# Four of fifteen row offsets of banded products as two 32x32 tiles in place of one 64x64 tile

## The reference

```python
x = x + L0_conv(ln(x))       # focal modulation: three depthwise convolutions of 3x3, 5x5, 7x7
t = t + L0_ffn(ln(t))        # a recurrence over the tokens: y = sigmoid(Wx + y V')
x = x + L1_conv(ln(x))       # a state-space mixer, forward and backward over the tokens
t = t + L1_ffn(ln(t))        # eight experts, the best two of each token
```

```python
for l, k in enumerate((k0, k1, k2)):
    ctx = gelu(dwconv_same(ctx, k))          # 3x3, then 5x5 on the result, then 7x7
    ctx_all = ctx_all + ctx * gates[..., l:l + 1]
```

## Time and profile before

| | us |
|---|---|
| median of 3 runs | 782.67 |
| lowest and highest run | 780.81 and 787.14 |
| profiled execution | 786.88 |
| span of its trace, first to last instruction | 785.1 |

### The profile page before, as it was taken

One profiled execution on the slowest core, in us unless ns is written; L12 is line 12 of the kernel. 1 busy time (PEld: TensorE's weight loads), 2 busy tenths in 40 slices (PEclk: granted clock), 3 DMA queues, 4 the chain that ended last, 5 costly groups with the idle time before them and its releaser, 6 DMA issues. The chain is left out here.

```text
span 785.1 us, 14059 instructions
## 1 busy us (share of the span) xinstructions
PE 635.6 (81%) x5604; PEld 400.8 (51%) x5610; DVE 623.2 (79%) x669; ACT 360.3 (46%) x567; POOL 470.0 (60%) x239
## 2 busy tenths in 40 slices
PE   7899669977837888888788789789789887885695
PEld 4787436644514555555455455456455554552242
DVE  3376874233319999999999999999999999977765
ACT  2222236653285566556556556556556564322000
POOL 2000000001018999999999999999999999960000
PEclk9999989986986999999999999999999999999777
DMA  9500000000355878779788878787877987800002
GB/s 371 224 3 3 1 2 1 1 2 2 92 121 131 205 199 232 194 201 233 193 199 228 201 202 215 212 203 204 222 201 199 227 202 198 224 14 1 1 12 52
DMA packets 35489, 110.43 MB, mean 141 GB/s; under 512 B 6816, under 2 KB 8992, under 8 KB 35040
## 3 DMA queue, kind: packets, MB, share of 16 engines
q1 hardware_dynamic: 35200, 108.71, 52.0%
q0 software_dynamic: 224, 0.83, 0.3%
HBM read 105.97 MB, written 3.54 MB: 139 GB/s over the span
## 5 line engine op out<-in xcount | busy, mean ns | idle before, releaser
L549 POOL TENSOR_TENSOR ring<-ring,big 128x1152 f32<-128x1152 f32 x74 | 193.7, 2631 | 4.0 <-DVE ring L922 4.0
L196 PE MATMUL banks<-ring,main_params 128*128 128x288 f32 x592 | 173.8, 422 | 0.6 <-POOL ring L549 0.6
L691 ACT ACTIVATE big<-big,small 128x576 f32<-128x576 f32 x192 | 142.5, 765 | 30.4 <-DVE ring L922 15.8
L922 DVE TENSOR_TENSOR_SCAN ring<-big,banks 128x576 f32<-128x576 f32 x111 | 146.1, 1340 | 1.5
L910 DVE TENSOR_TENSOR banks<-banks,big 128x576 f32<-128x576 f32 x192 | 141.2, 743 | 2.7 <-POOL big L535 1.6
L1260 PE MATMUL banks<-big,selectors 96*128 96x512 bf16 x192 | 72.7, 390 | 70.1 <-DVE ring L922 39.9
L196 PEld LDWEIGHTS banks<-ring,main_params 128*128 128x128 f32 x592 | 105.1, 191 | 36.1 <-issue 4.0
L525 POOL COPY big<-normed 128x288 f32<-128x288 f32 x8 | 3.0, 427 | 179.4 <-DVE normed L451 179.4
L549 POOL TENSOR_TENSOR normed<-normed,big 128x1152 f32<-128x1152 f32 x36 | 94.4, 2630 | 0.6 <-DVE normed L922 0.6
L691 ACT ACTIVATE banks<-big,small 128x576 f32<-128x576 f32 x64 | 47.5, 742 | 79.3 <-DVE ring L922 46.3
L196 PE MATMUL banks<-normed,main_params 128*128 128x288 f32 x288 | 83.5, 420 | 0.0
(11 more groups left out here) (186 smaller groups left out, 1002.2 us busy)
## 6 DMA issues: line engine op xcount, KB each, us to landing
big<-bc_rows SPq DMA_DIRECT2D x256, 288.0 KB, 4.4
big<-bc_rows SPq DMA_DIRECT2D x128, 144.0 KB, 4.4
big<-toeplitz_in SPq DMA_DIRECT2D x1, 3584.0 KB, 24.5
big<-toeplitz_in SPq DMA_DIRECT2D x1, 2560.0 KB, 15.2
bc_rows<-big SPq DMA_DIRECT2D x16, 144.0 KB, 3.6
big<-toeplitz_in SPq DMA_DIRECT2D x1, 1536.0 KB, 10.2
residual<-x_in SPq DMA_DIRECT2D x2, 576.0 KB, 5.8
out<-big SPq DMA_DIRECT2D x16, 72.0 KB, 1.8
```

Of the source, the lines that this page charges most:

```text
L196: last = nc.tensor.matmul(PS[rows, 2 * p + a, 0:HALF], lhsT, rhs[:, bass.ds(at + a * HALF, HALF)], start=start, stop=stop, skip_group_chec ...
L549: nc.gpsimd.tensor_tensor(slots, slots, CT[k % 5], ALU.mult).then_inc(weighted, 1)
L691: nc.scalar.activation(out, DT[b % 3], ACT.Exp, scale=ANEG[:, s:s + 1]).then_inc(decay_set, 1)
L922: nc.vector.tensor_tensor_scan(slot, DECAY[m % 3], place, 0.0, ALU.mult, ALU.add).then_inc(scanned, 1)
```

## The change

For four of the fifteen row offsets each 64x64 product is replaced by two 32x32 products, one for each block on the diagonal: strip b of the half's rows, weights of that block, and output partitions 64q + 32b to 64q + 32b + 31. Columns, bank, `start` and `stop` are those of the product replaced. The offsets are given by their place i in the order of `offsets(l)`: the second of level 0 (dy = -1), the third of level 1 (dy = 1), the third and the fifth of level 2 (dy = 1 and 2). All else stays, the layout of the weights in memory too.

```diff
@@ -246,6 +246,7 @@
         LINEAR = {(0, 1): ("q", 0), (1, 0): ("q", 1), (1, 1): ("global", 0), (2, 0): ("global", 1)}
+        SPLIT_AT = [(1,), (2,), (2, 4)]
         LINEARS = list(LINEAR.values())
@@ -1084,7 +1085,14 @@
                         for q in range(2):
                             at = TW_AT[l] + 64 * ((dy + KS[l] // 2) * CP + 2 * k + q)
                             dst = PS[64 * q:64 * (q + 1), 4 * kh + 2 * r + k % 4 // 2, k % 2 * COLS:(k % 2 + 1) * COLS]
-                            last = nc.tensor.matmul(dst.rearrange("p (m y) -> p m y", y=H)[:, :, ys], TW[rows, at:at + 64],
+                            dst = dst.rearrange("p (m y) -> p m y", y=H)[:, :, ys]
+                            if i in SPLIT_AT[l]:
+                                for b in range(2):
+                                    strip = slice(64 * r + 32 * b, 64 * r + 32 * (b + 1))
+                                    last = nc.tensor.matmul(dst[32 * b:32 * (b + 1)], TW[strip, at + 32 * b:at + 32 * (b + 1)],
+                                                            src[strip, 2 * k + q, :, there], start=i == 0, stop=i == KS[l] - 1)
+                                continue
+                            last = nc.tensor.matmul(dst, TW[rows, at:at + 64],
                                                     src[rows, 2 * k + q, :, there], start=i == 0, stop=i == KS[l] - 1)
                 return last
```

## The result

The changed kernel takes 794.23 us (median of 10 runs, 789.24 to 799.07), the kernel before 783.71 us beside it (10 runs, 780.64 to 787.14): a ratio of 1.0143, 95% interval 1.0111 to 1.0175, or 8.7 to 13.7 us more. The forecast was 10.2 us more. The profiled execution of the changed kernel took 799.07 us with a span of 797.3, the slowest of its runs.

What follows compares the result with a forecast made beforehand. TensorE, limited by streamed columns, was taken to bound the bands, with losses arriving whole. One of 32 splits falls into a hole; 31 x 0.33 = 10.2 us, added to the 782.67 median, gives 792.9 us, range 788 to 799.

Steps and rivals of the forecast that it cites:

- the bands: The banded products of L1087, one stretch from 27.6 to 69.4 us, TensorE busy for 41.33 of 41.80 us.
- A microsecond lost in the bands is a microsecond at the end: Behind the bands: nothing absorbs TensorE's loss, so the 10.2 us arrive whole in the total time.
- the stretches after it keep their lengths: Sign for the stages behind the bands: unchanged in length, while the bands' stretch grows from 41.7 to about 52 us.
- Instructions and loads cost nothing of their own: In the split passes: 256 more matmul records and 256 more loads cost no time; shorter loads gain nothing.
- The columns' price: TensorE's streaming in the bands: 0.87 ns a column, from 0.157 us a pass with a mean of 182 columns.
- The price of a split offset: Each split offset in the bands: two changes of tile form plus staggers, 0.11 + 0.06 + 0.13 + 0.03 = 0.33 us.
- The linear product of 41.86: L377 between bands, sixteen 32x32 tiles: same pair of form switches in the earlier trace, 0.38 us lost.
- The cover: The 0.43 us hole before 37.06, a wait for ScalarE's L570, takes up one split's 0.33 us; 31 remain.
- Rival 1, the switch is free: At the split offsets the array need not empty: nothing paid or gained, 782.7 us; chance 0.08.
- Rival 2, two strips take turns: Two strips of one 64-row half write one bank in turn, 0.16 us more per split pass: 803.1 us; chance 0.06.
- Rival 3, the clock: Stalls drop TensorE to 1.2 GHz for a while in the bands, 10 us more, some 803; chance 0.04.
- The estimate of 53 ns a switch: About 128 array cycles of drain at 2.4 GHz; 64 switches cost 3.4 us, 786.1 us in all; forecast rejected it.

Runs made afterwards that it cites:

- the short delay: Kernel before plus 9 idle 128x128 bf16 products ahead of the last half of level 2, bands untouched: ratio 1.0022 (0.9992 to 1.0053).
- the long one: Kernel before plus 44 idle 128x128 bf16 products ahead of the last half of level 2, bands untouched: ratio 1.0166 (1.0133 to 1.0199).
- level 0 alone: Against the kernel before, only the one offset of level 0 split into 32x32 tiles, 8 split offsets in place of 32: 790.69 us, ratio 1.007.
- the kernel with the same record counts and one tile form: Against the kernel before, the same four offsets as two products each, split by streamed columns, all tiles 64x64: 787.32 us, ratio 1.0009.
- all offsets small: Against the kernel before, all fifteen row offsets as two 32x32 tiles, no change of form left in the bands: 804.0 us, ratio 1.0259.
- the adjacent offsets: Changed kernel, but level 2 splits its third and fourth offsets, next to each other, not third and fifth: 793.58 us, ratio 1.0121 against the kernel before.
- one of 64x64 tiles: Against the kernel before, twelve offsets (all but each level's first) as two products each, split by columns, tiles kept 64x64: 802.17 us, ratio 1.021.

## Why the prediction was right

*What bounds the stage, and that the loss arrives whole.* Right in its main part: 9.51 us lost in the bands, a ratio that means 8.7 to 13.7 in the whole. "A microsecond lost in the bands is a microsecond at the end" holds for the short delay and is a little too low for the long one; the surplus of the changed kernel itself (11.2 by the ratio, 10.5 by the medians, against 9.5) is inside the interval. The sign "the stretches after it keep their lengths" did not hold in the profiled execution: the norms took 43.34 us for 41.77, at a lower granted clock, and only the 3 us allowed for the runs covered that. For level 0 alone, the 2.8 to 8.1 us stay unexplained: the short delay, as large in the bands, gave -0.6 to 4.2.

*Instructions and loads cost nothing of their own.* Right at this density, and shown by the kernel with the same record counts and one tile form (ratio 1.0009). The step rested on the spacing of 8 ns within one linear product, though, which is a burst and says nothing of a long run: with all offsets small, twice the instructions in the bands cost 17 us. The columns' price was taken as 0.87 ns; the stretch of eighty records gives 0.157 us / 182 = 0.86, which changes no term.

*The price of a split offset.* Forecast 0.11 + 0.06 + 0.13 + 0.03 = 0.33 us; measured at 38.1 us 0.11 + 0.05 + 0.14 + 0.02 = 0.32, and 0.32 again from the adjacent offsets. By the whole stretch it is (9.51 + 0.32) / 32 = 0.31. The linear product of 41.86 was the same pair of changes, and the only correction that it needed was half the stagger. That the two changes of form differ by 0.03 us matches the loads, 103 against 132 ns. The trace of before has a third length of load, 188 ns, into one 128x128 tile with 132 columns:

```profile
73.08 0.42 PE L1109 MATMUL banks<-big 128*32 128x288 f32 x4
73.43 0.38 PE L1129 MATMUL banks<-big 128*128 128x132 f32 x1
...
L1129 PEld LDWEIGHTS banks<-big x2: 186/188/189, 73.4 to 73.5; 128*128 128x128 f32 x2
```

There the first record ends at 73.81, 0.31 us after the last of the old form at 73.50; less 132 x 0.87 ns that is 0.20 us. So 0.10 to 0.11, 0.13 to 0.14 and 0.20 us were lost beside loads of 102 to 108, 132 and 188 ns: what a change of form costs, the stagger aside, is about the load of the new form, which does not run ahead across it. The length of the load was not varied by itself.

*The cover.* Before level 1 the hole was 0.43 us. In the changed kernel it is 0.11, as forecast: in narrow windows of the timeline the last four records of level 0 end at 40.94 + 0.34 = 41.28, and level 1 starts at 41.39:

```profile
40.94 0.34 PE L1095 MATMUL banks<-big 64*64 64x184 f32 x4
...
41.39 0.51 PE L1095 MATMUL banks<-big 64*64 64x192 f32 x5
```

*Rival 1, the switch is free*: fell. *Rival 2, two strips take turns*: fell, since both eights of a split offset end 0.15 us apart. So of the two pages of the Trainium skill, PSUM — Partial Sum Buffer, on bank collisions, which reports them for one bank and one quadrant, agrees with the trace (one bank, different quadrants, no turn taken); TensorEngine Tiling (Array Packing), Gotcha 1, as worded, does not. *Rival 3, the clock*: fell, 1.00 through the bands.

*The Trainium skill on the drain.* TensorEngine Tiling (Array Packing), Key Properties, says that a change of mode drains the engine; the trace agrees that such a change is paid, 0.11 and 0.14 us, for columns alone too. The estimate of 53 ns a switch that I made from TensorE: Matmul & The Clock Gate, Part 2, would have given 3.4 us; the measured 0.11 and 0.14 us are twice the 53 ns and more.

## What to carry to other kernels

Look for the same pair of operations elsewhere in the trace of before: one linear product gave the price of this change within a tenth, and each term within 0.01 us. A change of tile form, in rows and columns or in columns alone, cost 0.11 to 0.14 us here, about the length of the new form's weight load, and the stagger of the tiles comes on top; group products of one form and don't alternate. A tile split that keeps the streamed columns gained nothing here, where streaming is the bound, and it doubles the instructions of what is split.

## What the runs showed that was not expected

TensorE's supply of instructions. In two kernels, one of 32x32 and one of 64x64 tiles, that ran 128 matmuls with their loads in 2.6 to 3.3 us, TensorE stood idle for up to 1.3 us after each 128, and one 16 KB packet of the instruction queue went with each. In the bands at some 5 us for 128 (the kernel before, the changed one) there are none, and none either at 3.95 us for 128, the mean of the kernel with four offsets halved (1344 pairs in 41.5 us). Ahead of the bands the kernel before has one too, the 1.81 us in front of 24.03: 69 records follow it, and the kernels that stop early in the bands stop after 59 more, together 128.

The packets and the holes keep step. In the kernel with all offsets small, in the columns of the earlier trace rows:

```profile
59.70:59.80 0.10, 0.10 (x24) 1.00 0.58 164
...
60.70:61.90 1.20, 0.00 (x0) 1.00 0.00 0
...
63.00:63.10 0.10, 0.10 (x24) 1.00 0.63 164
```

A packet moves within 0.1 us, while TensorE still runs: here TensorE resumed 2.1 us after one, and the next moved 1.1 us after that. At the other such holes of the two kernels it is 2 to 3 us and 1 to 2 us. So the hole is not the transfer itself. That the packet is what TensorE waits for is read from this order and the counts, not tried by itself; what starts the fetch, what the 2.1 us are, and so what the longest run without a hole is, stay open.
